# Two reorderings inside a step: beta's squash ahead of rounding the state (ScalarE), the state's low part behind the masks (VectorE)

## The reference

```
x = x + _L0_xattn_ref(_layernorm(x), ctx, ctx, ...)
x = x + _L0_ffn_ref(_layernorm(x), ...)
x = x + _L1_xattn_ref(_layernorm(x), ctx, ctx, ...)
x = x + _L1_ffn_ref(_layernorm(x), ...)

# _L1_ffn_ref, for its tokens xf, twice (NUM_ITER = 2), v starts at zero:
ctx = concatenate([integrated, v])
shared_ctrl = gelu(ctx @ w_s1 + b_s1) @ w_s2 + b_s2
hidden = gelu(ctx @ expert_w1[e] + b1[e]); ctrl = hidden @ expert_w2[e] + b2[e]    # for the top 2 of 8 experts
# each control is split in alpha, beta, gate:
error = x - mu
v_next = sigmoid(alpha) * v - softplus(beta) * error
x_next = x + 0.1 * sigmoid(gate) * v_next
# x_next, v_next: weighted over shared and experts
halt = sigmoid(gelu(x_next @ w_h1 + b_h1) @ w_h2 + b_h2)
refined = gelu(x_next @ w_f1 + b_f1) @ w_f2 + b_f2
integrated = integrated + halt * refined * integration_weight
```

## Time and profile before

| | |
|---|---|
| median of 3 runs | 360.29 us (360.09 to 361.46) |
| time of the profiled execution | 360.35 us |
| its span (first to last instruction) | 358.6 us |
| busy: PE, PEld, DVE, ACT | 327.8, 231.2, 286.8, 196.1 us |
| mean granted clock of TensorE | 0.981 of full speed |

### The profile page before, as it was taken

One profiled execution on the slowest core, in us unless ns is written; L12 is line 12 of the kernel. 1 busy time (PEld: TensorE's weight loads), 2 busy tenths in 40 slices (PEclk: granted clock), 3 DMA queues, 4 the chain that ended last, 5 costly groups with the idle time before them and its releaser, 6 DMA issues.

```text
span 358.6 us, 4382 instructions
## 1 busy us (share of the span) xinstructions
PE 327.8 (91%) x1513; PEld 231.2 (64%) x1521; DVE 286.8 (80%) x602; ACT 196.1 (55%) x309; POOL 17.4 (5%) x20
## 2 busy tenths in 40 slices
PE   4989999899888788699798999999999999999996
PEld 4754886455554566477476677777677777777663
DVE  0547766655767778979998999999998998899694
ACT  2500034385637384286786686774845846734744
POOL 0040011202010112000000000000000000000000
PEclk9989999999999999789899999999999999999999
DMA  7999920000000000000000000000000000000001
GB/s 255 426 421 296 336 117 0 1 3 0 0 2 0 1 2 0 0 0 3 1 0 2 0 0 2 0 0 2 1 0 3 0 0 0 31 0 0 31 1 59
DMA packets 10869, 17.87 MB, mean 50 GB/s; under 512 B 352, under 2 KB 8800, under 8 KB 9568
## 3 DMA queue, kind: packets, MB, share of 16 engines
q1 hardware_dynamic: 10848, 17.60, 14.2%
HBM read 16.55 MB, written 1.05 MB: 49 GB/s over the span
## 4 chain that ended last, share of the span: by engine, by line
PE 51%; DVE 29%; issue 10%; ACT 4%; POOL 2%; DMA 2%; POOLq 1%; DVEq 0%; SPq 0%; ACTq 0%
PE ps L1195 47%; DVE zz L798 3%; DVE lst L783 2%; POOL lrs L359 2%; DVE ring L892 2%; DMA ctxT<-in_ctxT 2%; PE ps L1292 1%; DVE kv L1105 1%; DVE kv L1106 1%; DVE kv L1104 1%; DVE kv L1108 1%; PE ps L1271 1%; DVE wz L892 1%; DVE st L683 1%; DVE lmv L786 1%
## 5 line engine op out<-in xcount | busy, mean ns | idle before, releaser
L1195 PE MATMUL ps<-hm_odd,ew_hi 128*128 128x512 f32 (+1 forms) x164 | 52.3, 421 | 0.0
L1195 PE MATMUL ps<-hm_even,ew_hi 128*128 128x512 f32 (+1 forms) x160 | 49.8, 415 | 0.0
L1195 PEld LDWEIGHTS ps<-hm_odd,ew_hi 128*128 128x128 f32 (+1 forms) x164 | 29.1, 191 | 6.5 <-issue 0.5
L1195 PEld LDWEIGHTS ps<-hm_even,ew_hi 128*128 128x128 f32 (+1 forms) x160 | 27.5, 189 | 5.2
L1195 PE MATMUL ps<-hm_odd,ew_lo 128*128 128x512 f32 (+1 forms) x80 | 28.9, 398 | 0.0
L1195 PE MATMUL ps<-hm_even,ew_lo 128*128 128x512 f32 (+1 forms) x80 | 28.0, 390 | 0.0
L479 ACT ACTIVATE hid<-ps,pB 128x512 f32<-128x512 f32 x32 | 21.7, 687 | 10.5 <-PE ps L1195 9.9
L1195 PE MATMUL ps<-x_hi,w1x_hi 128*128 128x512 f32 x40 | 20.0, 499 | 5.6 <-ACT hid L479 3.9
L798 DVE TENSOR_SCALAR zz<-ps,lmv,lrs 128x128 f32<-128x128 f32 x48 | 16.4, 403 | 7.7 <-POOL lrs L359 7.5
L892 DVE SCALAR_TENSOR_TENSOR ring<-ring,pB,hid 128x1024 f32<-128x1024 bf16 x16 | 20.5, 1282 | 0.9
L783 DVE BATCH_NORM_STATS2 lst<-ps 128x6 f32<-128x128 f32 x48 | 10.7, 284 | 11.9 <-PE ps L1271 11.8
(11 more groups left out here) (286 smaller groups left out, 738.4 us busy)
## 6 DMA issues: line engine op xcount, KB each, us to landing
ring<-in_fc1b SPq DMA_DIRECT2D x4, 1024.0 KB, 17.0
ring<-in_fc2a SPq DMA_DIRECT2D x4, 1024.0 KB, 9.2
packC<-in_packC SPq DMA_DIRECT2D x1, 1152.0 KB, 9.3
pB<-in_packB SPq DMA_DIRECT2D x1, 1141.5 KB, 10.2
ctxT<-in_ctxT SPq DMA_DIRECT2D x2, 512.0 KB, 6.4
xtok<-in_xtok SPq DMA_DIRECT2D x1, 1024.0 KB, 9.1
xT<-in_xT SPq DMA_DIRECT2D x1, 1024.0 KB, 11.1
a<-in_fc1a SPq DMA_DIRECT2D x1, 1024.0 KB, 13.0
```

What stands on the lines that cost most here:

```text
L1195: return pe.matmul(out, lhsT, rhs, start=start, stop=stop)
```

## The change

Two calls change their place within their engine's program; no instruction is added, removed or resized. The programs of TensorE, GpSimd and the queues are the same row for row.

```diff
@@ ScalarE, the loop over steps
                 if s >= 2:
                     refine2(s - 2)
+                squashed(s, BETA)
                 if s + 2 < STEPS:
                     state_high(s + 2)
-                squashed(s, BETA)
                 if s >= 1:
                     refine1(s - 1)
@@ VectorE, hidden_masked(s, next_state)
                 kept(s, 2)
-                if next_state:
-                    state_split(s + 1)
                 lower(s, 0)
                 lower(s, 1)
                 kept(s, 3)
                 lower(s, 2)
+                if next_state:
+                    state_split(s + 1)
                 shared_halves(s)
                 lower(s, 3)
```

## The result

Over 22 runs of each, the changed kernel takes 361.49 us (360.94 to 362.16) and the kernel before 360.3 us. The ratio is 1.0029 (95% interval 1.0022 to 1.0036): 1.0 us slower by the ratio (the medians are 1.2 apart), and inside the forecast's range. The profiled execution has a span of 360.0 us and a mean clock of 0.981. One of the 12 executions of a later experiment, e8, took 646.56 us instead of some 360 and is left out of its ratio.

A forecast was written before the change was run, and what follows sets the result against it. TensorE sets the end, with VectorE full too. Late by 1.75 us in pass 2 and 2.20 in pass 3, less 0.89 in pass 4, plus 0.1 for ties: +1.4, 361.7 us; 8-in-10 range 360.5 to 363.4.

The forecast's parts named there:

- VectorE's part: Low parts moved behind the third masks: `v_lo` ends later, so TensorE starts `hidden(4)` in pass 2 1.75 us late.
- The hand-over: Time from VectorE's end of `v_lo` to TensorE's first load at `hidden`, taken as 0.36 us from `hidden(1)`.
- Pass 3: Second wait of 1.0 us at `hidden(5)`, delay then 2.20; the 0.55 won at `halt_a` is lost in it.
- Pass 4: TensorE's wait of 0.89 us at `halt_a` goes away and stays won, leaving the delay at +1.3.
- ScalarE's part: Beta's squash ahead of the roundings: gelu of `refine1` comes in time, removing the `halt_a` waits of 0.55 and 0.89 us.
- the ties: At `halt_a` ScalarE's gelu and TensorE arrive about together; 0.1 us of wait added for passes 4 and 5 together.
- The sum: Total over all passes: +1.4 us, a median of 361.7 us, 0.4% above before.
- the forecast's own span: Forecast total for shorter or longer hand-overs and ties: +0.8 to +1.8 us, or 361.1 to 362.1.
- The clock did not fall: Rival: TensorE's clock falls after the wait at `hidden(4)`, losing 1.7 us of full speed; +3.0, 363.3 us; chance 0.17.
- `hidden` did wait: Rival claimed the opposite: `v_lo` in time, no wait at `hidden`, only the `halt_a` gains; -1.4, 358.9 us; chance 0.05.
- the gelus were in time: Rival claimed the opposite: gelus of `refine1` stay late at `halt_a`, pass 4 wins nothing; +2.2, 362.5 us; chance 0.12.
- only the first wait: Rival: TensorE waits at `hidden(4)` but not at `hidden(5)`, and both `halt_a` gains count; +0.3, 360.6 us; chance 0.11.

The follow-up runs named there:

- e8: Kernel before with beta's squash put ahead of the roundings from pass 2 on only, VectorE unchanged: ratio 0.9976, -0.9 us.
- e5: As e3, but in pass 2 alone the low parts stand behind the third masks: ratio 1.0002 to the kernel before, +0.1 us.
- e2: Kernel before with VectorE's half alone, the low parts moved behind the third masks, ScalarE unchanged: ratio 1.0024, +0.9 us.
- e1: Kernel before with ScalarE's half alone, beta's squash ahead of the roundings in all passes, VectorE unchanged: ratio 1.0032, +1.2 us.
- e7: Changed kernel with the low parts one place earlier, between third `kept` and third `lower`: ratio 0.9966 to the kernel before, -1.2 us.
- e6: Changed kernel with the low parts moved behind all masks, after the last `lower`: ratio 1.0228 to the kernel before, +8.2 us.
- e3: Changed kernel with the low parts moved up to after the second `lower`, ScalarE's half kept: ratio 0.9961 to the kernel before, -1.4 us.
- e4: As e3, but in pass 3 alone the low parts stand behind the third masks: ratio 1.0016 to the kernel before, +0.6 us.
- e9: Kernel before with the low parts moved to after the second `lower`, ScalarE unchanged: ratio 0.9986, -0.5 us.

## Why the prediction was right

- **VectorE's part.** Right in kind and place: both new waits stand where forecast, at `hidden(4)` and `hidden(5)`, and nowhere else. The term was a little too large: 1.75 forecast, 1.46 measured. The hand-over is 0.17 to 0.19 and not 0.36, and `v_lo` starts 0.72 ahead of L948 and not 0.60. The 0.36 was a right reading of `hidden(1)`, and comes again there in the changed kernel; but it did not carry over to the later passes. The clock was at 0.75 on average from 145 to 150 in the kernel before; whether that makes the difference is not shown.
- **Pass 3.** Forecast 2.20 late at `hidden(5)`, measured 1.72. Of the 0.48 too much, 0.19 is the hand-over; the rest is that `v_lo` ends 0.29 earlier than reckoned, mostly because VectorE was not 0.22 late (`th` ended 0.11 ahead of the start of L1148, with TensorE less late than forecast). That what is won at `halt_a` is lost again in the same pass held; e5 shows it from the other side.
- **Pass 4.** Forecast 0.89 won, measured 0.83 (from 1.72 late to 0.89).
- **ScalarE's part.** The chain from row tiles to squash (1.36 against 1.35) and from squash to gelu (3.96 against 1.62 + 1.06 + 1.29 = 3.97) held, and the ties cost nothing: the 0.1 that I added was not there. But the prediction credited the gain of pass 4 to this half, and that was wrong in its reason: e2 has the same gain without it. The step missed that TensorE's own lateness covers a wait for something that hangs on VectorE. The total didn't suffer by it only because both halves were in the change; for either half alone the same working would have given a wrong number.
- **The sum.** +1.4 forecast, +1.0 measured by the runs and +0.90 by the trace. That is near the low end of the forecast's own span (+0.8), for the hand-over and the `th` that it had too large.
- **The rivals.** The clock did not fall (1.00 from 195 to 245). `hidden` did wait, in both passes, and the gelus were in time. The rival "only the first wait" is nearly what e5 makes by placing the low parts late in pass 2 alone: +0.1 against its +0.3.
- **What I overlooked.** The change's two halves are tied. With the roundings behind the squash the low parts must move as well, or VectorE waits in passes 0 and 1 (e1), unless those two passes keep the old order (e8). The low parts have room to move back only as far as just behind the last `kept` (e7). The change moved them two instructions too far.

## What to carry to other kernels

When a producer's instruction is moved back in its queue, compute when it will end in each pass and compare it with when its consumer wants it; here a place that costs next to nothing and one that costs 2 us are two instructions apart. Don't price the parts of a change one by one where engines wait for each other in turn: a wait removed is worth something only as long as its engine isn't made late by another, and lateness in two consecutive passes can count for little more than that of one (here 1.4 and 2.0 alone, 2.2 together). Passes with less work (here 0 and 1, with no v) need their own check, since a wait there can put a full engine behind for several passes.

## What the runs showed of the hardware that I had not expected

**Where the clock falls is a matter of the execution.** In each of ten traces (before, after and all but e6) TensorE waits 2.64 or 2.65 us for L479 in pass 1, as in the earlier trace rows. In six of them the granted clock is 0.83 on average from 173 to 183, in the other four (e3, e4, e7, e9) it is 1.00. Here the kernel before and e3:

```profile
173.00:183.00 10.00, 9.32 (x40) 7.06 (x40) 9.79 (x11) 6.61 (x12) 0.00 (x0) 0.83 0.00 1
```

```profile
173.00:183.00 10.00, 8.11 (x40) 6.15 (x42) 9.76 (x11) 7.86 (x12) 0.00 (x0) 1.00 0.00 1
```

0.17 x 10 is 1.7 us of TensorE's full speed. The four did not save it: from 145 to 160 they had 0.66 where the kernel before had 0.77 (0.11 x 15 = 1.65 us), and the mean clock of the kernel before and of e3 is 0.981. The program doesn't decide it: e3, e4 and e5 are the same up to pass 2, and e5 fell at 173 while e3 and e4 did not. Their row tiles of pass 2 start at 203.83, 203.84 and 204.46, which is 0.6 us apart. So single spans can't be compared here at the level of 1 us; a stretch behind that place can.

TensorE's waits of 1.28 us (before), 1.35 us (after) and 1.85 us (e4, at `hidden(5)`) left the clock at 1.00, and the 3.58 and 3.30 us waits of e6 were each followed by a fall. The Trainium skill (TensorE: Matmul & The Clock Gate, "What's actually happening") says that the clock gate's activity window is free-running and doesn't reset when a kernel starts, so that the point of a transition varies with where the first matmul falls in it. That the same program fell at different times in e3 and e5 fits that; no trace shows the window itself.

**The order of unchanged instructions on VectorE is worth 0.19 us a pass** (23.47 against 23.66 us, e9 against before), with the same operations and sizes. The interval from L910 to its successor, 1.15 or 1.33 us, holds nearly all of it.
